# First part of a two-block transformer kernel: VectorE operands in PSUM, one activation table in the opening, split row loads, new slots

## The chip, the cores and the metric

One core of one Trainium2 chip. The time is the device time of one launch in microseconds (us). Before the change it was 2034.73 us, the median of 3 runs (2034.38 to 2038.0).

## The reference

The input is x of 8 x 256 x 128, called eight samples of 256 tokens here. Two blocks follow each other. `_layernorm(x) * (1 + scale) + shift` and a gate come from the condition c by an adaLN modulation; a gate's magnitude is kept at 0.25 or more. The kernel computes, for each sample:

```python
# block 0, attention: features relu(q rw), relu(k rw); no softmax
kv  = einsum('bhsf,bhsd->bhfd', kp, v); out = (qp kv) / (qp sum(kp) + EPS)
# block 0, experts: 8 dense experts, gelu, weights of the two best gates
h = gelu(x @ W_in[e] + b_in[e]); out += combine[e] * (h @ W_out[e] + b_out[e])
# block 1, sparse attention over x itself
probs = softmax(x x^T / sqrt(D)); vacuum = probs < 0.01
attended = (kept probs / their sum) x;   + 0.01 * sum(vacuum probs) * W
# block 1, "late": 6 layers of local attention (16 heads of 64, windows of 32,
# l2-normed and rotated q and k), each with a gated gelu feed-forward
```

The modulation multiplies silu(c) by a 128 x 768 matrix for each block.

## The kernel before

Activations stand transposed, 128 features on the partitions, 256 tokens of one sample in the free dimension. Three kinds of jobs run: `attention(b)` (block 0's attention), `experts(b)` (experts and then the sparse attention and the last layer norm of the first part) for b = 0 to 7, and `late(u)` for 48 units, u = 8 * layer + sample. The first part is the 16 jobs of the first two kinds; the late part follows, and the two overlap a little, since sample 0 can start before sample 7 is done.

Each engine has its own program, and in it the order of all jobs is written by hand through slots: a job is a generator that moves from step to step at given slots (`PE_A`, `ACT_B`, `DVE_AT` and so on), and `interleave` merges the jobs by slot number. The slots are no times: they only give the order of instructions on each engine. Engines meet through semaphores (`wait_ge`, `then_inc`). `settle` is a wait of an engine for its own last instruction.

PSUM has eight banks. In the first part `Banks.take` hands them out in a ring: the ninth request gets the first bank again, and TensorE waits until that bank's user has signalled. In the late part three banks form such a ring.

The opening: ACT issues 13 small loads of rows (biases, gains and the two conditions, `row_loads`), copies the four turned parts of x out of PSUM (L887), and waits for `cols`, all 105 rows turned by TensorE in one transposition (L432). Then `silu` on ACT (L899) with its own activation table, six products per block (`modulation`, L439), and on VectorE some fifteen small instructions from L1196 to L1207 that build scale, shift and gate. Only then does VectorE enter `attention(0)`, since it waits for `mod` ahead of the first layer norm. Block 1's silu and modulation and the constants `wcT` and `wsum` are made in `prepare_block1` when `experts(0)` starts.

A layer norm is one pattern on four engines: TensorE mean (L459), VectorE subtraction (L1230), ACT square (L906), TensorE variance (L463), ACT ln and exp (L910, L911), VectorE product with that (L1234, both operands in SBUF) and scale and shift (L1242, SBUF to SBUF). L893 is the load of the table that has ln and exp.

The sparse attention: TensorE scores of sample b in the bank `s1` (L614), VectorE maximum (L1383), ACT exp into the SBUF tile `e_prob` (L996), VectorE division by the sum (L1390), twice two selections with sums (L1395, L1397; signal `sp`), TensorE transposition (L623), ACT copy (L1002), TensorE product (L631), VectorE L1413 and L1416.

In the late part, per half c of a unit: ACT copies q and k (L1019, `raw`) and squares them (L1027), VectorE sums (L1455, `ss`), turns them by sine (L1468, `sin`), POOL turns them by cosine (L1665, `cos`) and adds both (L1674, `add`), VectorE normalises (L1476, `nrm`), TensorE transposes (L690, `tqk`). The softmax is `smax` (L1489, L1490), `exp` (L1060), `ssum`. The tables of the rotation are made by L1439 and L1440 in unit 0.

SP issues loads of x, of weights and constants; POOL splits weights into two parts (L1603, L1604) chunk by chunk, and SP loads chunk i only when chunk i - 2 is split.

## Time and profile before

| what | before |
|---|---|
| median of 3 runs | 2034.73 us |
| the profiled execution's own time | 2035.73 us |
| its span, first to last instruction | 2034.4 us |
| TensorE busy | 1875.6 us (92%) |
| VectorE, ACT, POOL busy | 1576.5, 1606.5, 1068.7 us |
| mean granted TensorE clock | 0.984 |

The span is what the rows below add up to; 1.3 us of the profiled execution lie around it. Busy TensorE time is modelled from pipelined instructions, so it counts a slowly clocked or queued product as busy. The first part takes about the first fifth of the span.

### The profile page before, as it was taken

The page shows a single profiled execution, that of the slowest core. Times are in us where ns is not written, and L with a number is a line of the kernel's source. Part 1 is how long each engine was busy: PE and PEld are TensorE (multiplying, and loading weights), DVE is VectorE, ACT ScalarE, POOL GpSimd, SP SyncE. Part 2 cuts the span into 40 slices and gives each one's busy share as a digit, 9 for nine tenths or more (in the row PEclk, how much of TensorE's full clock was granted, in tenths as well). Part 3 has the DMA queues.
Part 4 walks back from the last instruction along what each step waited for, and adds up shares of the span by engine and source line. Part 5 has one row for each costly group of instructions (what it writes and reads, how often), then busy time and mean ns, then how long its engine had stood idle before and what let it go on. Part 6 is the DMA issues. An engine that isn't in the chain of part 4 may idle for free.

```text
span 2034.4 us, 78899 instructions
## 1 busy us (share of the span) xinstructions
PE 1875.6 (92%) x34796; PEld 1571.9 (77%) x34796; DVE 1576.5 (77%) x2244; ACT 1606.5 (79%) x2840; POOL 1068.7 (53%) x523
## 2 busy tenths in 40 slices
PE   4999999768999999999999999999999999999986
PEld 3789998656777777778778778777778787878775
DVE  4565655568888888878788888888888888889874
ACT  2577777557888888888888888888888888888864
POOL 3100000256567666677575766656765668666430
PEclk9899999889999999999999999999999999999999
DMA  5000000023434333243433343333434334342331
GB/s 170 7 12 5 5 7 6 2 81 87 115 82 126 98 106 112 80 127 85 114 94 115 92 127 100 107 104 90 122 91 124 88 94 129 98 115 80 103 80 43
DMA packets 119822, 174.01 MB, mean 86 GB/s; under 512 B 25303, under 2 KB 44346, under 8 KB 119482
## 3 DMA queue, kind: packets, MB, share of 16 engines
q1 hardware_dynamic: 119308, 168.92, 30.0%
q8 instruction: 275, 4.51, 0.9%
q14 instruction: 65, 0.53, 0.1%
q10 hardware_dynamic: 174, 0.05, 0.0%
HBM read 117.54 MB, written 51.38 MB: 83 GB/s over the span
## 4 chain that ended last, share of the span: by engine, by line
PE 63%; DVE 20%; issue 7%; POOL 5%; ACT 4%; ACTq 0%; DMA 0%; POOLq 0%; DVEq 0%
PE bank L690 7%; PE s_pair L712 6%; PE bank L667 5%; PE bank L669 5%; PE bank L668 5%; DVE bank L1455 5%; DVE rt L1476 4%; DVE t L1468 4%; PE o_pair L741 4%; PE bank L724 4%; PE bank L753 3%; PE bank L862 3%; DVE sm L1489 2%; PE s_pair L594 2%; POOL rt L1665 2%
## 5 line engine op out<-in xcount | busy, mean ns | idle before, releaser
L1665 POOL TENSOR_TENSOR rt<-raw,rot 128x1024 f32<-128x1024 f32 x192 | 456.0, 2375 | 318.1 <-PE bank L690 259.0
L1674 POOL TENSOR_TENSOR rt<-rt,t 128x2048 f32<-128x2048 f32 x96 | 439.4, 4578 | 184.3 <-DVE t L1468 180.2
L667 PE MATMUL bank<-wqkv_hi,xs 128*128 128x512 f32 x576 | 252.8, 439 | 7.6 <-ACT vn L1036 2.8
L1489 DVE TENSOR_REDUCE sm<-s_pair 128x16 f32<-128x1024 f32 x96 | 117.6, 1225 | 182.1 <-PE s_pair L712 178.8
L1019 ACT ACTIVATE raw<-bank 128x512 f32<-128x512 f32 x384 | 229.1, 598 | 29.2 <-PE bank L669 5.0
L690 PE MATMUL bank<-const,rt 128*128 128x128 f32 x1536 | 209.2, 279 | 32.7 <-DVE rt L1476 29.5
L668 PE MATMUL bank<-wqkv_lo,xs 128*128 128x512 f32 x576 | 228.5, 397 | 1.2 <-issue 1.2
L1476 DVE TENSOR_TENSOR rt<-rt,bank 128x2048 f32<-128x2048 f32 x96 | 219.6, 2288 | 12.1 <-POOL rt L1674 9.1
L669 PE MATMUL bank<-wqkv_hi,xs 128*128 128x512 f32 x576 | 228.8, 397 | 0.0
L1468 DVE TENSOR_TENSOR t<-raw,bank 128x1024 f32<-128x1024 f32 x192 | 224.8, 1211 | 0.6
L1455 DVE TENSOR_REDUCE bank<-t 128x32 f32<-128x2048 f32 x96 | 219.4, 2286 | 5.8 <-ACT t L1027 5.7
L690 PEld LDWEIGHTS bank<-const,rt 128*128 128x128 f32 x1536 | 170.7, 142 | 68.4 <-issue 49.2
L1027 ACT ACTIVATE t<-raw 128x2048 f32<-128x2048 f32 x96 | 184.8, 1926 | 7.6 <-POOL rt L1674 6.5
L840 PE MATMUL bank<-oT,wo 128*128 128x256 f32 x768 | 173.7, 379 | 0.9 <-DVE hh L1514 0.9
L712 PE MATMUL s_pair<-kT,qT 64*32 64x64 f32 x12288 | 157.1, 226 | 13.9 <-issue 13.9
L712 PEld LDWEIGHTS s_pair<-kT,qT 64*32 64x32 f32 x12288 | 131.8, 106 | 46.0 <-issue 35.6
L741 PE MATMUL o_pair<-v,pT 64*32 64x64 f32 x12288 | 147.8, 225 | 17.8 <-issue 17.8
L741 PEld LDWEIGHTS o_pair<-v,pT 64*32 64x32 f32 x12288 | 128.5, 105 | 45.8 <-issue 45.8
L840 PEld LDWEIGHTS bank<-oT,wo 128*128 128x128 f32 x768 | 145.4, 190 | 22.7 <-DVE hh L1514 1.1
L1053 ACT ACTIVATE kT<-bank 128x512 f32<-128x512 f32 x192 | 104.8, 596 | 72.8 <-PE bank L690 69.8
L1047 ACT ACTIVATE qT<-bank 128x512 f32<-128x512 f32 x192 | 104.3, 597 | 69.8 <-PE bank L690 69.8
L1633 POOL TENSOR_TENSOR e_hs<-e_h_b,e_hs 128x256 fp32r<-128x256 f32 x8 | 5.8, 727 | 283.2 <-ACT e_hs L959 283.2
(363 smaller groups left out, 4467.0 us busy)
## 6 DMA issues: line engine op xcount, KB each, us to landing
v<-v_rows SPq DMA_DIRECT2D x288, 256.0 KB, 4.5
v_rows<-vn SPq DMA_DIRECT2D x192, 256.0 KB, 3.8
v<-v_rows SPq DMA_DIRECT2D x96, 192.0 KB, 3.4
wraw<-in_L_ffn_Wqkv_dram SPq DMA_DIRECT2D x36, 256.0 KB, 3.1
wo<-in_L_ffn_Wo_dram SPq DMA_DIRECT2D x6, 512.0 KB, 4.8
wraw<-in_L_ffn_W_in_dram SPq DMA_DIRECT2D x8, 256.0 KB, 3.7
w_out<-in_L_ffn_W_out_dram SPq DMA_DIRECT2D x8, 256.0 KB
wraw<-in_L_ffn_W_dram SPq DMA_DIRECT2D x12, 170.5 KB, 2.3
```

The costliest lines, as they stand in the source:

```text
L667: pe.matmul(bank[:, :], hi, w[0][:, :], start=True, stop=False)
L668: pe.matmul(bank[:, :], hi, w[1][:, :], start=False, stop=False)
L669: return pe.matmul(bank[:, :], lo, w[0][:, :], start=False, stop=True)
L690: e = pe.transpose(bank[:, i * P:(i + 1) * P], k.rt_r[c][:, at:at + P], k.ident)
L712: e = pe.matmul(k.s_pair[WIN * g:WIN * (g + 1), at:at + 2 * WIN], qT[rows, hp, WIN * g:WIN * (g + 1)], k.kT_r[u % 2][rows, hp, k0:k0 + 2 * ...
L741: e = pe.matmul(k.o_pair[WIN * g:WIN * (g + 1), at:at + DH], k.pT_r[c][rows, hp, WIN * g:WIN * (g + 1)], k.v2_r[c][rows, g, hp * DH:(hp + ...
L840: e = pe.matmul(bank[:, 0:S], k.wo[:, n, :], k.oT_r[u % 2][:, n, :], start=(n == 0), stop=(n == INNER // P - 1))
L1455: dve.tensor_reduce(k.rn_p[c], heads(k.t2[:, :]), AX.X, ALU.add).then_inc(s["sq_sum"], 1)
L1468: e = dve.tensor_tensor(pairs(k.t2[:, part]), pairs(k.raw_r[c][:, part])[:, :, ::-1, :], sinv, ALU.mult)
L1476: dve.tensor_tensor(v, v, k.rn_p[c].unsqueeze(2).to_broadcast([P, 2 * HEADS, DH]), ALU.mult)\
L1665: e = pool.tensor_tensor(heads(k.rt_r[c][:, part]), heads(k.raw_r[c][:, part]), cosv, ALU.mult)
L1674: pool.tensor_tensor(k.rt_r[c][:, :], k.rt_r[c][:, :], k.t2[:, :], ALU.add).then_inc(s["rot_add"], 1)
```

## The change

It changes the first part's code and every slot table. The arithmetic stays the same but for the form of silu and of the gates.

- Rows: `bq, bk, bo, c0, c1` get a tile `rows_f` and a signal of their own (`ld_first`, 5 loads); the other 8 loads go to `rows_m`, five of them ahead of the copies of x, three behind. POOL clears `rows_m` instead of VectorE.
- Opening: ACT loads one table (ln, exp) at once. silu is computed as c / (1 + exp(-c)): exp on ACT, three instructions on VectorE, for both blocks together. The mean and the subtraction of `attention(0)` stand ahead of the modulation; TensorE turns the rest of x and the early rows after the first mean, and makes modulation(0) after the first variance. The gate needs six VectorE instructions instead of fifteen.
- PSUM operands: ACT writes the exp of a layer norm and the exp of the sparse softmax back into their banks, and VectorE's next steps read and write there. The variance's bank is held until the layer norm's end, the bank `s1` until `sp`.
- Loads: block 1's modulation matrix and `w_c` come behind the first two chunks; the eight `w_out` tiles alternate with chunks and have two signals of their own.
- Slots: all tables are new.

```diff
-ATTENTION_START, ATTENTION_SPACING = 0, 40
-EXPERTS_START, EXPERTS_SPACING = 63, 40
-LATE_START, LATE_SPACING = 399, 32
+ATTENTION_START, ATTENTION_SPACING = 2, 40
+EXPERTS_START, EXPERTS_SPACING = 65, 40
+LATE_START, LATE_SPACING = 398, 32
...
-DVE_B = dict(ln_sq_b=0, ln_sd_b=12, ln_out_b=15, top2=18, weights=19, combine=30, expert0=33, expert1=35, expert2=38,
-             expert3=44, expert4=44, expert5=54, expert6=54, expert7=56, expert8=59, moe_out=60, ln_sq_c=60,
-             ln_sd_c=71, ln_out_c=77, scores=77, exp=81, threshold=81, spT=92, attend=96, back=97, ln_sq_d=97,
-             ln_sd_d=102, ln_out_d=102)
...
+DVE_B = dict(ln_sq_b=0, ln_sd_b=9, ln_out_b=13, top2=19, weights=20, combine=22, expert0=30, expert1=40, expert2=43,
+             expert3=48, expert4=53, expert5=57, expert6=58, expert7=60, expert8=64, moe_out=67, ln_sq_c=67,
+             ln_sd_c=80, ln_out_c=82, scores=82, exp=84, threshold=84, spT=95, attend=99, back=102, ln_sq_d=102,
+             ln_sd_d=111, ln_out_d=111)
...
-ACT_AT = dict(xs=0, qk00=9, qk01=10, qk02=11, qk03=12, sq0=20, qk10=20, norm0=29, qk11=30, qk12=35, qk13=35, sq1=36,
-              norm1=41, v00=41, v01=44, v10=46, v11=48, tqk00=49, tqk01=49, tqk02=61, tqk03=61, tqk10=64, tqk11=64,
-              tqk12=65, tqk13=67, exp0=73, tp00=77, tp01=78, exp1=96, tp10=100, tp11=102, to00=104, to01=104,
-              to10=114, to11=117, xf=129, lnsq=135, rstd=137, gelu0=150, gelu1=150, gelu2=153)
-DVE_AT = dict(ss0=15, sin0=21, nrm0=29, ss1=33, sin1=38, nrm1=58, smax0=60, ssum0=76, smax1=79, oa0=91, ssum1=92,
-              oa1=108, z_mid=124, xc=127, hn=134, hh0=144, hh1=145, hh2=145, z_out=160)
...
+ACT_AT = dict(xs=0, qk00=7, qk01=9, qk02=9, qk03=10, sq0=14, qk10=16, norm0=25, qk11=28, qk12=33, qk13=33, sq1=34,
+              norm1=39, v00=39, v01=42, v10=43, v11=43, tqk00=43, tqk01=45, tqk02=55, tqk03=56, tqk10=61, tqk11=63,
+              tqk12=65, tqk13=65, exp0=71, tp00=75, tp01=75, exp1=92, tp10=98, tp11=99, to00=101, to01=103, to10=108,
+              to11=112, xf=128, lnsq=132, rstd=134, gelu0=146, gelu1=148, gelu2=151)
+DVE_AT = dict(ss0=17, sin0=26, nrm0=32, ss1=38, sin1=40, nrm1=60, smax0=64, ssum0=75, smax1=81, oa0=93, ssum1=95,
+              oa1=106, z_mid=126, xc=133, hn=136, hh0=146, hh1=146, hh2=153, z_out=162)
...
+    def prepare_block0():
+        turn_x(1)
+        columns(0, k.rows_f, FIRST_ROWS, (s["ld_first"], 16 * k.n_first_dma), ("silu", 2))
+        turn_x(2)
+        turn_x(3)
...
+        if b == 0 and tag == "a":
+            prepare_block0()
         yield from t.to("ln_sq_" + tag)
-        bank = bank_for(("var", tag, b), "ln_sd_" + tag, b + 1)
+        bank = bank_for(("var", tag, b), "ln_out_" + tag, b + 1)
         pe.wait_ge(s["ln_sq_" + tag], b + 1)
         pe.matmul(bank[:, 0:S], k.ones_d[:, :], xsq, start=True, stop=True).then_inc(s["ln_var_" + tag], 1)
+        if b == 0 and tag == "a":
+            modulation(0)
...
-        bank = bank_for(("s1", b), "exp1", b + 1)
+        bank = bank_for(("s1", b), "sp", b + 1)
...
+    exp_ln()
+    for dst, src in k.first_loads:
+        act.dma_start(dst, src).then_inc(s["ld_first"], 16)
+    act.wait_ge(s["ones"], 2)
+    for dst, src in k.row_loads[:ROWS_BEFORE]:
         act.dma_start(dst, src).then_inc(s["ld_rows"], 16)
     for q in range(NT // P // 4):
         act.wait_ge(s["pe_x"], q + 1)
         act.activation(k.xT[:, q * 512:(q + 1) * 512], k.work.at["x", q][:, :], ACT.Copy).then_inc(s["xT"], 1)
+        if q == 1:
+            at = ROWS["c0"][0]
+            act.wait_ge(s["cols"], 1)
+            act.activation(k.work.at["cols", 0][:, at:at + 2 * B], k.cols[:, at:at + 2 * B], ACT.Exp, scale=-1.0)\
+                .then_inc(s["silu"], 1)
+    for dst, src in k.row_loads[ROWS_BEFORE:]:
+        act.dma_start(dst, src).then_inc(s["ld_rows"], 16)
...
-        act.activation(sq, sq, ACT.Exp, scale=-0.5).then_inc(s["ln_sd_" + tag], 1)
+        act.activation(k.work.at["var", tag, b][:, 0:S], sq, ACT.Exp, scale=-0.5).then_inc(s["ln_sd_" + tag], 1)
...
+    def silu():
+        at = ROWS["c0"][0]
+        c, e = k.cols[:, at:at + 2 * B], k.work.at["cols", 0][:, at:at + 2 * B]
+        dve.wait_ge(s["silu"], 1)
+        settle(dve.tensor_scalar(e, e, 1.0, None, ALU.add))
+        settle(dve.reciprocal(e, e))
+        dve.tensor_tensor(k.silu[:, :], c, e, ALU.mult).then_inc(s["silu"], 1)
...
+        dve.tensor_copy(mod[:, 0::3, :], raw[:, 0::3, :])
+        dve.tensor_scalar(mod[:, 1::3, :], raw[:, 1::3, :], 1.0, None, ALU.add)
+        settle(dve.tensor_scalar(mag, raw[:, 2::3, :], -1.0, 0.25, ALU.mult, ALU.max))
+        settle(dve.tensor_tensor(mag, mag, raw[:, 2::3, :], ALU.max))
+        settle(dve.scalar_tensor_tensor(out=twice, in0=raw[:, 2::3, :], scalar=0.0, in1=mag,
+                                        op0=ALU.is_ge, op1=ALU.mult))
+        dve.scalar_tensor_tensor(out=mod[:, 2::3, :], in0=twice, scalar=2.0, in1=mag,
+                                 op0=ALU.mult, op1=ALU.subtract).then_inc(s["mod"], 1)
...
-        settle(dve.tensor_tensor(xc, xc, sd, ALU.mult))
+        if b == 0 and tag == "a":
+            dve.wait_ge(s["mod"], 1)
+        settle(dve.tensor_tensor(xn, xc, xn, ALU.mult))
...
-        dve.tensor_scalar(dst, xc, gain, shift, ALU.mult, ALU.add).then_inc(s["ln_out_" + tag], 1)
+        dve.tensor_scalar(dst, xn, gain, shift, ALU.mult, ALU.add).then_inc(s["ln_out_" + tag], 1)
...
-        for c in range(TC):
-            e = dve.tensor_scalar(pr[:, c, :], pr[:, c, :], one(RS, c), None, ALU.mult)
-        settle(e)
         if b:
             dve.wait_ge(s["pe_spT"], b)
         for c in range(TC):
-            settle(dve.scalar_tensor_tensor(out=spb[:, c, :], in0=pr[:, c, :], scalar=THRESH, in1=pr[:, c, :],
-                                            op0=ALU.is_lt, op1=ALU.mult, accum_out=one(VAC, c)))
-            e = dve.scalar_tensor_tensor(out=spb[:, c, :], in0=pr[:, c, :], scalar=THRESH, in1=pr[:, c, :],
-                                         op0=ALU.is_ge, op1=ALU.mult, accum_out=one(SPS, c))
+            e = dve.tensor_scalar(spb[:, c, :], pr[:, c, :], one(RS, c), THRESH, ALU.mult, ALU.is_ge)
+        settle(e)
+        for c in range(TC):
+            e = dve.scalar_tensor_tensor(out=spb[:, c, :], in0=pr[:, c, :], scalar=one(RS, c), in1=spb[:, c, :],
+                                         op0=ALU.mult, op1=ALU.mult, accum_out=one(SPS, c))
+        settle(e)
+        for c in range(TC):
+            e = dve.scalar_tensor_tensor(out=pr[:, c, :], in0=pr[:, c, :], scalar=one(RS, c), in1=spb[:, c, :],
+                                         op0=ALU.mult, op1=ALU.subtract, accum_out=one(VAC, c))
         e.then_inc(s["sp"], 1)
...
+    sp.dma_start(k.wmod[1][:, :], a["L1_wmod"]).then_inc(s["ld_wmod1"], 16)
+    sp.dma_start(k.w_c[:, :], a["L1_attn_W"]).then_inc(s["ld_moe"], 16)
     for e in range(NE):
+        if 2 + e < NE:
+            load_chunk(2 + e)
         sp.dma_start(k.w_out[:, e, :, :], a["L0_ffn_W_out"][e].rearrange("(m p) n -> p m n", p=P))\
-            .then_inc(s["ld_moe"], 16)
+            .then_inc(s[f"ld_out{e // (NE // 2)}"], 16)
```

## Rows read from the trace of the kernel before

**Rows 1.** Windows: us, then busy us of PE, PEld, DVE, ACT, POOL, PEclk, DMA, GB/s.

```profile
66.00:335.00 269.00, 268.15 (x2430) 242.86 (x2431) 156.50 (x502) 203.17 (x417) 14.61 (x18) 1.00 0.03 7
...
400.00:475.00 75.00, 45.51 (x795) 36.11 (x796) 56.76 (x58) 40.50 (x68) 48.57 (x23) 0.78 0.24 68
...
500.00:1960.00 1460.00, 1391.53 (x29285) 1152.22 (x29284) 1242.08 (x1421) 1242.01 (x2131) 954.18 (x434) 1.00 0.38 103
```

**Rows 2.** Timeline of the opening: start, us, engine, line, operation, [idle before, releaser].

```profile
8.07 2.07 ACT L887 ACTIVATE xT<-bank 128x512 f32<-128x512 f32 x4
10.81 0.43 PE L432 MATMUL s_pair<-const,rows_m 105*128 105x105 f32 x1 [2.24 <-DMA rows_m<-in_L_c_dram]
11.94 2.70 PE L439 MATMUL s_pair<-silu,wmod 128*128 128x8 f32 x12 [0.69 <-ACT silu L899]
14.68 0.21 DVE L1196 COPY mod<-s_pair 128x48 f32<-128x48 f32 x1 [3.12 <-PE s_pair L439]
21.43 0.42 DVE L1230 TENSOR_TENSOR e_ln_a<-xT,o_pair 128x256 f32<-128x256 f32 x1
...
23.67 1.28 ACT L893 ACT_TABLE_LOAD   x1 [1.30 <-PE o_pair L463]
...
26.38 0.72 DVE L1242 TENSOR_SCALAR e_h_a<-e_ln_a,mod 128x256 f32<-128x256 f32 x1
```

**Rows 3.** The same timeline, from the end of attention(0) to the first expert.

```profile
44.18 0.43 DVE L1304 TENSOR_TENSOR xT<-xT,e_oT 128x256 f32<-128x256 f32 x1
...
52.61 1.06 PE L459 MATMUL bank<-xT,ones_d 128*128 128x256 f32 x2
...
66.62 0.39 PE L584 MATMUL bank<-e_hs,w_in_hi 128*128 128x256 f32 x1
```

**Rows 4.** Timeline of the steady first part around one use of the bank s1.

```profile
117.39 1.03 PE L614 MATMUL bank<-e_h_c 128*128 128x256 f32 x4
119.69 1.95 PE L594 MATMUL s_pair<-w_out,e_hid 128*128 128x128 f32 x16
...
123.33 1.95 PE L594 MATMUL bank<-w_out,e_hid 128*128 128x128 f32 x16
...
125.64 0.08 DVE L1397 DVE_READ_ACCUMULATOR e_sp<-e_prob 128x1 f32 x1
```

**Rows 5.** VectorE instructions by line: ns min/median/max, first and last start.

```profile
L1390 DVE TENSOR_SCALAR e_prob<-e_prob,e_small x16: 346/353/4652, 123.4 to 399.4; 128x256 f32<-128x256 f32 x16
L1242 DVE TENSOR_SCALAR e_h_b<-e_ln_b,mod x8: 411/412/414, 59.6 to 342.1; 128x256 f32<-128x256 f32 x8
L1302 DVE TENSOR_SCALAR e_oT<-s_pair,cols,mod x5: 543/544/546, 108.4 to 276.3; 128x256 f32<-128x256 f32 x5
L1476 DVE TENSOR_TENSOR rt<-rt,bank x96: 2286/2289/2290, 411.4 to 1965.6; 128x2048 f32<-128x2048 f32 x96
```

**Rows 6.** Timelines of POOL, VectorE, TensorE and ACT where the parts meet.

```profile
394.60 4.77 POOL L1665 TENSOR_TENSOR rt<-raw,rot 128x1024 f32<-128x1024 f32 x2 [9.65 <-DVE rot L1440]
396.99 7.10 DVE L1390 TENSOR_SCALAR e_prob<-e_prob,e_small 128x256 f32<-128x256 f32 x2
399.45 4.49 POOL L1674 TENSOR_TENSOR rt<-rt,t 128x2048 f32<-128x2048 f32 x1
410.85 1.09 PE L623 MATMUL s_pair<-const,e_sp 128*128 128x128 f32 x4 [16.61 <-DVE e_sp L1397]
412.59 1.91 ACT L1027 ACTIVATE t<-raw 128x2048 f32<-128x2048 f32 x1
420.63 4.58 POOL L1674 TENSOR_TENSOR rt<-rt,t 128x2048 f32<-128x2048 f32 x1 [10.22 <-DVE t L1468]
```

**Rows 7.** One late unit: ACT's timeline, then TensorE in the critical chain.

```profile
1021.81 0.58 ACT L1019 ACTIVATE raw<-bank 128x512 f32<-128x512 f32 x1
1022.28 1.05 ACT L1060 ACTIVATE p<-p 128x1024 f32<-128x1024 f32 x1
...
1023.62 0.87 PE bank L690 x8
```

More of the change, by code:

```diff
@@ L200 @@
 SIGNALS = (
-    "ones zero rf xT cols silu mod cst wsum w_split "
+    "ones rf xT cols silu mod cst wsum w_split "
     "pe_x pe_setup "
@@ L423, in pe_program, with turn_x @@
     pe.wait_ge(s["ld_ident"], 16)
-    for q in range(NT // P // 4):
+    def turn_x(q):
         bank = bank_for(("x", q), "xT", q + 1)
@@ L429, in pe_program, with columns @@
         e.then_inc(s["pe_x"], 1)
-    bank = bank_for("cols", "cols", 1)
-    pe.wait_ge(s["ld_rows"], 16 * k.n_rows_dma)
-    pe.transpose(bank[:, 0:NROWS], k.rows_m[0:NROWS, :], k.ident[0:NROWS, 0:NROWS]).then_inc(s["pe_setup"], 1)
+    turn_x(0)
+    def columns(n, rows, count, loaded, free):
+        bank = bank_for(("cols", n), *free)
+        pe.wait_ge(*loaded)
+        pe.transpose(bank[:, 0:count], rows[0:count, :], k.ident[0:count, 0:count]).then_inc(s["pe_setup"], 1)
     def modulation(n):
@@ L880, in shifted @@
         return act.activation(dst[DH:P, 1:S], src[DH:P, 0:S - 1], ACT.Copy)
-    act.wait_ge(s["zero"], 1)
-    for dst, src in k.row_loads:
-        act.dma_start(dst, src).then_inc(s["ld_rows"], 16)
-    for q in range(NT // P // 4):
-        act.wait_ge(s["pe_x"], q + 1)
-        act.activation(k.xT[:, q * 512:(q + 1) * 512], k.work.at["x", q][:, :], ACT.Copy).then_inc(s["xT"], 1)
-    act.wait_ge(s["cols"], 1)
     table = {"set": None}
@@ L1212, in dve_program, with columns @@
-    modulation(0)
+    def columns(n, first, count, ready):
+        dve.wait_ge(s["pe_setup"], ready)
+        dve.tensor_copy(k.cols[:, first:first + count], k.work.at["cols", n][:, 0:count]).then_inc(s["cols"], 1)
+    def silu():
[5 more added lines that the diff above has]
+        dve.tensor_tensor(k.silu[:, :], c, e, ALU.mult).then_inc(s["silu"], 1)
@@ L1411, in experts @@
             dve.wait_ge(s["pe_atT"], b)
+        parts = [bank[:, c * D:(c + 1) * D] for c in range(TC)]
         for c in range(TC):
-            e = dve.tensor_scalar(o[:, c, :], bank[:, c * D:(c + 1) * D], one(SPS, c), None, ALU.mult)
+            e = dve.tensor_scalar(parts[c], parts[c], one(SPS, c), None, ALU.mult)
         settle(e)
         for c in range(TC):
-            e = dve.scalar_tensor_tensor(out=o[:, c, :], in0=k.wsum[:, :], scalar=one(VAC, c), in1=o[:, c, :],
+            e = dve.scalar_tensor_tensor(out=o[:, c, :], in0=k.wsum[:, :], scalar=one(VAC, c), in1=parts[c],
                                          op0=ALU.mult, op1=ALU.add)
@@ L1779, in sp_program @@
     load_down(0)
-    for i in range(2, NE + 2 + NCHUNK_LATE):
+    for i in range(NE, NE + 2 + NCHUNK_LATE):
         load_chunk(i)
@@ L1873, in row_loads @@
     rows("c1", a["L1_c"], B)
-    return out
+    return first, out
 class Chunks:
```

169 lines of the change are left out of this document (80 added, 89 removed).

## Prediction

> **What bounds the kernel now.** I read the windows first, then the timelines of the places where TensorE is not full, then the chain of waits of one late unit. The reader is to see three stretches in the windows [rows 1]. From 66 to 335 us TensorE is busy 268.15 of 269.00 us at clock 1.00: there only TensorE's own work counts, and faster VectorE instructions are worth nothing. Ahead of 66 us it waits for chains through all engines [rows 2, 3]. Where the parts meet, 400 to 475 us, it is idle 29.5 us, at a mean clock of 0.78. In the late part, 500 to 1960 us, it is idle 68.5 of 1460 us, about 1.5 us in each unit of some 32 us (48 units in 1559 us). The change can gain in the opening and at the meeting point, can lose in the full stretch, and can do either in the late part through the slots alone.
>
> **The opening, before the first h.** Today the rows land at 10.81, all 13 loads of them. The modulation products end at 11.94 + 2.70 = 14.64, and VectorE works on gates from 14.68 until the first subtraction at 21.43. The first h is there at 26.38 + 0.72 = 27.10, that is 5.7 us after that subtraction, with a table load of 1.28 in between [rows 2].
>
> After the change the subtraction needs only the first part of x. ACT issues 10 loads ahead of the copies instead of 13, and has no table load there; its first copy, at 8.07 behind 13 issues and a load of the length of 1.28, comes at about (8.07 - 1.28) x 10 / 13 = 5.2, and with the table load somewhere ahead I take 5.6, the mean at 7 and the subtraction at 8. The first rows (five loads, issued first) I take as landed at 8.5: nearest row 10.81, for the last of 13 loads. TensorE then turns them and the last two parts of x until 10.5; ACT waits for the turned columns between its second and third copy, so exp, two copies (2.07 / 4 each), three load issues (6.8 x 3 / 13 = 1.6) and the square queue behind that wait: the square comes at 12.8. So the variance is made at 13.3 to 14.5 and the modulation, queued behind it, until 14.5 + 2.7 = 17.2. VectorE's six gate instructions take 1.6 (0.21 each, and four waits for itself). Two layer norm instructions of 0.43 and 0.72 at most end h at 19.9. **Gain 7.2 us.** If the rows land no sooner than now, 10.81, everything from the transposition on is 2.3 later and the gain is 4.9. If the modulation were done when it is now, 14.64, it is 9.7. The new wait of VectorE for `mod`, ahead of the product, has nothing but this chain behind it.
>
> **The preparation of block 1.** From the end of attention(0), 44.18 + 0.43 = 44.6, to the mean of experts(0) at 52.61 pass 8.0 us, and the first expert starts at 66.62 [rows 3]. Gone are silu's table load (1.28), the wait for silu, half of the gate instructions (some 1 us) and the reload of the ln and exp table for that layer norm (1.28); new are one transposition of the late rows and its copy, 0.43 and some 0.3, partly beside the products. The rest of the waits stands. I take 3.3 us; bounds 1.3 (one load) and 5. SP's `w_out` loads now queue behind the waits for splits; they are needed from the first expert on, at 56, and at some 3 us per pair of loads from 15 on (an estimate) all are in by 40. Opening together: **-10.5 us**, from -6 to -14.
>
> **The full stretch.** TensorE's own work stays the same. Two banks are held longer. The bank s1 is written by 117.39 + 1.03 = 118.4, and `sp`, which now frees it, comes at 125.7, 7.3 us later [rows 4]. The new VectorE order has the same six instructions, but two of them read PSUM, which adds some 0.5 us: 7.8. In the new order eight requests behind s1 are two experts (three banks each), the variance of the next experts job and the first of four banks for the q features. One expert takes about (123.33 - 119.69) - 0.43 = 3.2 us [rows 4], so the eighth request comes after 6.4 + 0.4 = 6.8 us. That is 1.0 us too soon, in seven samples at most, and everything of TensorE is queued behind that wait: +7. It is 0 if ACT and VectorE run a microsecond ahead. I take the middle, **+4 us**. The variance's bank is asked for again after eight requests, too, but its owner needs only a further 0.8 us of VectorE, ahead of that point; I cost it at nothing, and it costs the same per sample if VectorE is behind.
>
> A VectorE instruction also gets slower by the move: a scale and shift out of SBUF takes 412 ns, one with a PSUM operand of the same size 544 ns [rows 5]. 32 of the first and 16 of L1390 (353 ns) move: 32 x 0.13 + 16 x 0.19 = 7.2 us of VectorE, bounds 0 and 7.2. VectorE is busy 156.50 of 269 us in the full stretch, so I take nothing for it beyond the 0.5 us in the sum above. The Trainium skill, VectorE: DVE Perf Modes, section Why PSUM operands drop a tier, speaks against the change here: PSUM has one read port for VectorE, so a fp32 `tensor_scalar` with a PSUM operand falls back to one element a cycle. By the page each of those 48 would take up to twice its time, and on the path they would make the sum 19 us longer, an estimate. The rows price the step at 544 / 412 = 1.3 for the scale and shift and at most 544 / 353 = 1.5 for L1390 [rows 5], and the measured durations are used.
>
> **Where the parts meet.** For the last sample the two divisions take 7.10 us together instead of 2 x 0.353, and the six instructions from 396.99 to 410.8 take 13.8 us, where the same six of sample 0 run from 123.4 to 125.7, in 2.3 [rows 4 to 6]: POOL's rotation and sum run beside them, 394.60 to 399.4 and 399.45 to 403.9 [rows 6]. TensorE stood idle 16.61 us for it. With PSUM operands I take them at 3.4 us, since L1476, one operand in PSUM, keeps to 2286 to 2290 ns in all 96 cases, those beside POOL's work among them [rows 5]. What is late next is POOL's own sum at 403.94: ACT's second square, which came at 412.59 behind the selections' copy, needs just that. So [rows 6] 412.59 - 403.94 = 8.65 us go, and the next POOL sum, now at 420.63, follows by the same amount. The new slots put VectorE's rotation of unit 0 ahead of the last sample's h, and ACT's first square ahead of its squares: POOL's 394.60 moves to about 391.5, 3 us more, against 2 us by which the last sample's own chain is later, which is now covered. **-11.7 us**; bounds -5 (another wait takes half) and -17 (all of the idle 16.61).
>
> **The late part.** Slots swap neighbours: on TensorE one transposition pair, the feed-forward's down product and the mean; on VectorE the layer's end ahead of the subtraction; on ACT the second exp ahead of the copy of `qk11`; SP's and POOL's splits and loads move at layer ends only. I find no wait on which TensorE stands that any of these moves by more than its slack, and take 0, with 8 us either way (0.17 us per unit).
>
> **Sum:** -10.5 + 4 - 11.7 + 0 = -18.2 us on the profiled span of 2034.4, which becomes 2016.2; with the 1.3 us around it 2017.5 against 2035.73. The median is 1.0 below that execution: 2016.5.
>
> **Rivals.**
> (1) The bank s1 stalls in full and the layer norm banks with it: 2 us in each of seven samples, 14 instead of 4. For it speaks that TensorE has no idle time to hide it; against it, that the swap of slots may have put VectorE's part ahead. 2026.5.
> (2) The opening gives only what the gate instructions gave, because the small loads land late behind x: -5 instead of -10.5: 2022. For it: ten loads share the queues with 1 MB of x.
> (3) The meeting point gains more or less: POOL's sum is not next, but the idle 16.61 us go as a whole, or the rotation ahead of h costs what it gains: 2011 or 2023.
> (4) Slower: ACT's second exp, 1.05 us, ahead of the copy of `qk11`. The copy now starts at 1021.81 and takes 0.58; behind the exp it ends at about 1023.4, and the transpositions at 1023.62 hold the second that reuses its bank 0.4 later [rows 7]. The margin is 0.6 us. If ACT is later than in this unit by that, TensorE waits in every unit; it decides from 0.39 us per unit on (18.2 / 47), and with 0.45 us it is +21: 2038.
> (5) The slower PSUM reads lie on the path, 7.2 us of VectorE in all: 2023.7. The Trainium skill's section named above states the rule behind this rival. VectorE's 58% share in the full stretch speaks against it.
> (6) The change does not do what it says: VectorE still waits beside POOL at the meeting point, 2025.
>
> **How the numbers follow.** A measurement of this kernel tells about 0.2%, 4 us, from no change. Chances: forecast (2010 to 2021) 0.42; (1) 0.12; (2) 0.12; (3) 0.14; (4) 0.08; (5) 0.04; (6) 0.04; 0.04 left for more gain than I count. The range takes the forecast's own bounds, (2), (3), (5), (6) and most of (1): 2001 to 2030. Faster by over 4 us is all but (4) and a part of (1): 0.88. Within 4 us 0.05, slower 0.07.
>
> **What the changed profile would show.** The first subtraction near 8 and the first h near 20; the first expert product near 56; no table load between the start and that expert's gelu; the full stretch without TensorE waits on VectorE or, if I am right about s1, about seven waits of under 1 us ahead of the q features; the six selections of the last sample in 3 to 4 us, and POOL's second sum some 20 us earlier than 420.63; the same late part, shifted. The forecast is wrong if the late units take another time than now, or if the first expert starts at 60 or later.

## The result, and the profile after

Two sets of 20 runs have medians of 2036.1 us before and 2041.92 us after. The ratio of the two, with its 95% interval, is 1.0022 [1.0012, 1.0033]: slower by about 4.5 us, just past the 0.2% that the prediction took as the bound. The forecast was 2016.5, with a range of 2001 to 2030 and 0.88 on faster. It was wrong in sign and outside its range. The profiled execution has a span of 2039.2 us and took 2040.55.

The windows of the changed kernel (columns as in [rows 1], with the number of instructions behind each busy time) show where TensorE lost time:

```profile
66.00:335.00 269.00, 255.29 (x2322) 230.25 (x2318) 157.99 (x487) 195.30 (x396) 14.66 (x18) 1.00 0.03 7
...
400.00:475.00 75.00, 49.22 (x748) 38.21 (x749) 54.51 (x61) 41.57 (x75) 45.26 (x22) 0.78 0.24 69
500.00:1960.00 1460.00, 1383.58 (x29307) 1155.03 (x29289) 1239.89 (x1417) 1240.29 (x2125) 955.64 (x435) 1.00 0.37 103
```

In the full stretch TensorE is busy 255.29 of 269 us, where it was 268.15 [rows 1]: 13 us of new idle time, at an unchanged clock of 1.00. The rest of the text follows four milestones: the end of `attention(0)`, the residual additions that end each sample's experts (`x2`), VectorE's first rotation product of the late part (`nrm0`, L1507), and the first late output (unit 0's last step on VectorE, L1600). The table is put together from the starts in VectorE's timeline of both kernels, in us; `x2` (L1395) has eight starts, one per sample.

```
                 attention(0)  x2 first   x2 last   last-first   nrm0    nrm0 - x2 last   first late output
before               44.18      103.08    382.50      279.42    411.44       28.94             535.53
after                34.12       94.95    386.54      291.59    412.00       25.46             538.22
difference          -10.06       -8.13     +4.04      +12.17     +0.56       -3.48              +2.69
```

The books balance: -8.1 at the first `x2`, +12.2 over seven samples, -3.5 to `nrm0`, +2.1 from there to the first late output is +2.7; another +2.1 comes in 47 further units, and the span is 4.8 longer.

**The opening** came as it was said, and somewhat better up to the first h. These are lines of the changed kernel's timeline, columns as in [rows 2]:

```profile
0.74 1.28 ACT L903 ACT_TABLE_LOAD   x1 [0.74 <-PEq L1965]
...
7.58 0.42 DVE L1252 TENSOR_TENSOR e_ln_a<-xT,bank 128x256 f32<-128x256 f32 x1 [7.58 <-PE bank L470]
...
12.86 2.08 PE L445 MATMUL o_pair<-silu,wmod 128*128 128x8 f32 x12
...
16.52 0.54 DVE L1271 TENSOR_SCALAR e_h_a<-o_pair,mod 128x256 f32<-128x256 f32 x1
...
55.52 0.39 PE L599 MATMUL bank<-e_hs,w_in_hi 128*128 128x256 f32 x1
```

The first subtraction starts at 7.58 instead of 21.43, the first h is there at 17.06 instead of 27.10, and the first expert's product starts at 55.52 instead of 66.62 [rows 2, 3].

**The full stretch** has waits on TensorE that were not there. TensorE's waits from 100 to 335 us in the changed kernel (us in total, times, longest):

```profile
PE bank L580 <- DVE e_gate L1368: 4.8, 5, 1.3
PE s_pair L517 <- DVE s_pair L1427: 4.7, 5, 0.9
PE s_pair L611 <- DVE zT L1271: 1.9, 4, 0.5
```

and the longest of the kernel before in the same view:

```profile
PE bank L601 <- DVE e_acc L1362: 0.4, 1, 0.4
```

The second line is the bank `s1`, which the q features of `attention` (L517) ask for again. Its own place, from the timelines of TensorE and VectorE in the changed kernel:

```profile
240.84 1.03 PE L631 MATMUL s_pair<-e_h_c 128*128 128x256 f32 x4
...
248.14 0.60 PE L476 MATMUL bank<-e_ln_b,ones_d 128*128 128x256 f32 x2
249.67 0.48 PE L517 MATMUL s_pair<-e_qkT,w_rf 32*128 32x256 f32 x2 [0.93 <-DVE s_pair L1427]
```

The scores end at 241.87; `sp` releases the bank 7.8 us later, and the q features that reuse it wait 0.93 us.

From the first to the last `x2` TensorE's waits add up to 14.3 us: 5.6 for gates (L580, six times), 6.3 for `s1`, 2.4 for banks of the layer norms.

**The meeting point** has short selections and a new hold. POOL, VectorE and TensorE in the changed kernel, columns as in [rows 6]:

```profile
393.67 4.77 POOL L1696 TENSOR_TENSOR rt<-raw,rot 128x1024 f32<-128x1024 f32 x2 [4.68 <-DVE rot L1471]
398.52 4.53 POOL L1705 TENSOR_TENSOR rt<-rt,t 128x2048 f32<-128x2048 f32 x1
405.41 0.72 POOL L1718 TENSOR_TENSOR xs<-zT,xs 64x256 fp32r<-64x256 f32 x1 [2.36 <-ACT xs L897]
...
406.92 4.79 POOL L1696 TENSOR_TENSOR rt<-raw,rot 128x1024 f32<-128x1024 f32 x2
419.12 4.56 POOL L1705 TENSOR_TENSOR rt<-rt,t 128x2048 f32<-128x2048 f32 x1 [7.41 <-DVE t L1499]
```

```profile
400.15 2.93 DVE L1412 TENSOR_SCALAR e_small<-e_small 128x2 f32<-128x2 f32 x1
...
404.36 0.88 DVE L1420 TENSOR_SCALAR e_sp<-s_pair,e_small 128x256 f32<-128x256 f32 x2
...
407.20 2.10 DVE L1431 TENSOR_SCALAR e_small<-e_small 128x2 f32<-128x2 f32 x1
...
409.42 2.32 DVE L1433 TENSOR_SCALAR e_small<-e_small 128x2 f32<-128x2 f32 x1
...
412.00 2.29 DVE L1507 TENSOR_TENSOR rt<-rt,bank 128x2048 f32<-128x2048 f32 x1
```

```profile
407.31 1.09 PE L640 MATMUL s_pair<-const,e_sp 128*128 128x128 f32 x4 [5.37 <-DVE s_pair L1427]
```

The 256-wide selections no longer wait. But three `tensor_scalar`s over **two** elements in each partition (128x2), which scale the negated maximum, add 1e-9 and multiply by 0.01, take 2.93, 2.10 and 2.32 us. How long they take elsewhere stands in VectorE's groups by line (ns min/median/max):

```profile
L1420 DVE TENSOR_SCALAR e_sp<-s_pair,e_small x14: 474/480/484, 113.3 to 404.8; 128x256 f32<-128x256 f32 x14
L1423 DVE SCALAR_TENSOR_TENSOR e_sp<-s_pair,e_small,e_sp x14: 478/482/485, 114.2 to 405.7; 128x256 f32<-128x256 f32 x14
...
L1412 DVE TENSOR_SCALAR e_small<-e_small x8: 169/170/2926, 110.2 to 400.1; 128x2 f32<-128x2 f32 x8
L1416 DVE RECIPROCAL e_small<-e_small x8: 165/166/166, 113.1 to 404.2; 128x2 f32<-128x2 f32 x8
L1431 DVE TENSOR_SCALAR e_small<-e_small x8: 169/170/2100, 116.1 to 407.2; 128x2 f32<-128x2 f32 x8
L1432 DVE RECIPROCAL e_small<-e_small x8: 165/166/166, 116.3 to 409.3; 128x2 f32<-128x2 f32 x8
L1433 DVE TENSOR_SCALAR e_small<-e_small x8: 147/149/2324, 116.4 to 409.4; 128x2 f32<-128x2 f32 x8
```

The instructions with a PSUM operand keep to 484 and 485 ns; the two-element `tensor_scalar` out of SBUF goes from 170 to 2926. For L1420 these rows are no test, since POOL idles from 403.05 to 405.41, just where the last pair runs. The test is the same instruction in r11_last_sample_again, described below, where it runs from 389.81 on and POOL's pair from 387.41 to 392.20:

```profile
L1437 DVE TENSOR_SCALAR e_sp<-s_pair,e_small x2: 474/479/484, 389.8 to 390.2; 128x256 f32<-128x256 f32 x2
```

Each of the three slow ones ends where an instruction of POOL ends: 400.15 + 2.93 = 403.08 is the end of the sum L1705 (403.05), 407.20 + 2.10 = 409.30 is the middle of the pair L1696, and 409.42 + 2.32 = 411.74 its end (406.92 + 4.79 = 411.71). `nrm0` comes behind both, at 412.00. The Trainium skill, SBUF — State Buffer, section Who interferes with whom, has this as an exclusive lock on the port pair that VectorE's two-port mode shares with GpSimd, with the second to issue blocked for the whole instruction; these rows agree. The prediction had priced this wait on the wide instructions only. The reciprocal L1432 runs between two of them, beside the same pair, and keeps to 166 ns.

### The profile page after: what moved, and what is told of

The parts are those of the page before. It is cut to its first block, busy times and chain, and to the rows that moved or that the text cites. A ratio compares the mean times of both kernels' runs of the same rounds, so it can differ in the third digit from the quotient of the medians.

```text
span 2039.2 us, 78883 instructions
## 1 busy us (share of the span) xinstructions
PE 1874.3 (92%) x34797; PEld 1579.7 (77%) x34797; DVE 1573.3 (77%) x2229; ACT 1604.3 (79%) x2835; POOL 1070.2 (52%) x524
## 3 DMA queue, kind: packets, MB, share of 16 engines
q8 instruction: 275, 4.51, 0.9%
## 4 chain that ended last, share of the span: by engine, by line
PE 60%; DVE 21%; issue 8%; ACT 6%; POOL 5%; DMA 0%; ACTq 0%; POOLq 0%; DVEq 0%; SPq 0%
PE bank L707 7%; PE s_pair L729 6%; PE bank L684 6%; PE bank L686 5%; PE bank L685 5%; DVE rt L1507 4%; DVE bank L1486 4%; PE o_pair L758 4%; DVE t L1499 4%; PE bank L741 4%; PE bank L770 3%; PE bank L879 3%; DVE sm L1520 2%; POOL rt L1705 2%; POOL rt L1696 2%
## 5 line engine op out<-in xcount | busy, mean ns | idle before, releaser
L1696 POOL TENSOR_TENSOR rt<-raw,rot 128x1024 f32<-128x1024 f32 x192 | 456.4, 2377 | 328.0 <-PE bank L707 288.2
L1705 POOL TENSOR_TENSOR rt<-rt,t 128x2048 f32<-128x2048 f32 x96 | 439.7, 4580 | 163.1 <-DVE t L1499 159.0
L707 PE MATMUL bank<-const,rt 128*128 128x128 f32 x1536 | 219.3, 281 | 34.6 <-DVE rt L1507 28.2
L1507 DVE TENSOR_TENSOR rt<-rt,bank 128x2048 f32<-128x2048 f32 x96 | 219.6, 2288 | 13.2 <-POOL rt L1705 10.0
L729 PEld LDWEIGHTS s_pair<-kT,qT 64*32 64x32 f32 x12288 | 132.3, 106 | 42.7 <-issue 32.1
L1066 ACT ACTIVATE qT<-bank 128x512 f32<-128x512 f32 x192 | 110.1, 599 | 67.2 <-PE bank L707 67.2
```

Source lines behind the costliest of these rows:

```text
L707: e = pe.transpose(bank[:, i * P:(i + 1) * P], k.rt_r[c][:, at:at + P], k.ident)
L729: e = pe.matmul(k.s_pair[WIN * g:WIN * (g + 1), at:at + 2 * WIN], qT[rows, hp, WIN * g:WIN * (g + 1)], k.kT_r[u % 2][rows, hp, k0:k0 + 2 * ...
L1507: dve.tensor_tensor(v, v, k.rn_p[c].unsqueeze(2).to_broadcast([P, 2 * HEADS, DH]), ALU.mult)\
L1696: e = pool.tensor_tensor(heads(k.rt_r[c][:, part]), heads(k.raw_r[c][:, part]), cosv, ALU.mult)
L1705: pool.tensor_tensor(k.rt_r[c][:, :], k.rt_r[c][:, :], k.t2[:, :], ALU.add).then_inc(s["rot_add"], 1)
```

## The experiments

Each was run beside the kernel before on the same chip; the medians of the kernel before on the three chips are 2036.8, 2033.99 and 2036.93 us, so ratios are compared, not medians. "Stretch" is the last `x2` less the first; "meeting" is `nrm0` less the last `x2`. Both come from one profile each, in us. What one profile can tell is seen from e8 and r11, which are the same kernel: they differ by 0.85 us in the stretch, by nothing at the meeting point, and by 2.5 us at the first late output.

```
kernel                      ratio [95%]               stretch   meeting   first late output
before                                                279.42    28.94     535.53
after                       1.0022 [1.0012, 1.0033]   291.59    25.46     538.22
e1_code_old_slots           1.0023 [1.0008, 1.0038]   301.31    22.45     540.39
e2_slots_old_code           1.0021 [1.0004, 1.0037]   282.21    25.85     541.38
e3_small_off_port           0.9961 [0.9946, 0.9976]   293.29    18.35     531.29
e4_s1_free_at_exp           0.9965 [0.9951, 0.9980]   285.96    25.88     530.20
e5_ln_banks_free            1.0001 [0.9987, 1.0015]   287.66    25.41     533.22
e6_all_banks_free           0.9953 [0.9937, 0.9969]   282.03    25.85     528.61
e7_opening_alone            0.9953 [0.9936, 0.9969]   279.69    28.92     526.65
e8_last_sample_old_slots    0.9941 [0.9923, 0.9959]   279.96    21.37     520.12
r9_last_sample_new_slots    0.9925 [0.9903, 0.9947]   281.96    18.16     520.97
r10_last_small_only         0.9953 [0.9938, 0.9968]   280.21    28.26     526.71
r11_last_sample_again       0.9926 [0.9903, 0.9948]   280.81    21.37     522.60
```

**Code and slots taken apart.** The first run is the changed code with the slot tables of before, the second the code of before with the new tables; the diff is the tables alone.

```diff
-PE_B = dict(ln_sq_b=6, ln_sd_b=6, ln_out_b=12, ...
+PE_B = dict(ln_sq_b=6, ln_sd_b=6, ln_out_b=15, ...
```

> The changed code with all slot tables of the kernel before. Changed kernel's profile: x2 of the samples comes 44.5 us apart instead of 42.0, and three TensorE waits per sample stand there: 0.9 to 1.3 us for the bank s1, 0.9 for the gate weights, 0.5 for the bank of the last layer norm. Theory S (order): most of the loss is the new slots, so here the spacing is 42 to 42.5 and the kernel keeps the opening's gain of 8 to 10 us: 2024 to 2030 where the kernel before has 2036. Theory B (banks held longer): the wait for s1 is there in any order, the spacing is 43 to 43.5, and the kernel is at 2031 to 2037. Theory D (VectorE slower by its PSUM reads): spacing 44 to 44.5 as in the changed kernel, 2040.

> The code before with all new slot tables. Theory S: the spacing of x2 is 43.5 to 44.5 with no gain in the opening, 2044 to 2052. Theory B: spacing 42.0 to 42.5 and 2036 to 2040. In both the opening's first h stays at 27.

Neither half is the gain or the loss: both are slower than before. The first came to 2041.21 us, near the number of theory D, but with the cause of theory B, and with 45.8 us from `x2` to `x2` where none had more than 44.5. The second came to 2041.54, between the two ranges, with nearly the spacing of theory B (42.2 to 42.7). With the old slots the changed code stretches to 301.31, and TensorE's waits from 100 to 335 us name all three held banks:

```profile
PE bank L599 <- DVE e_h_b L1271: 7.8, 5, 1.6
PE bank L599 <- DVE bank L1427: 4.7, 5, 0.9
PE s_pair L599 <- DVE e_h_c L1271: 2.6, 5, 0.5
```

L1271 is the end of a layer norm, which now frees the variance's bank, with 1.6 us a sample ahead of `experts(b)` and 0.5 us for the sparse block. So the new slots repair much of what the held banks cost: 9.7 us of the stretch. Of these, 2.7 are lost again ahead of the first `x2` (94.95 against 92.30). By themselves, with the old code, they cost 2.8 us in the stretch, at the gates (this is the view of the second run), and give 3.1 at the meeting:

```profile
PE bank L565 <- DVE e_gate L1341: 4.6, 5, 1.2
```

That alone would be no loss. But the first `x2` comes 3.0 us later too (106.04), and 3.2 more pass from `nrm0` to the first late output, which is 5.85 us behind that of the kernel before.

At the meeting point this run shows something that the prediction did not see. VectorE in e2_slots_old_code, and POOL's second pair there:

```profile
406.03 0.62 DVE L1390 TENSOR_SCALAR e_prob<-e_prob,e_small 128x256 f32<-128x256 f32 x2
...
408.90 2.44 DVE L1397 SCALAR_TENSOR_TENSOR e_sp<-e_prob 128x256 f32<-128x256 f32 x1
...
411.38 2.18 DVE L1401 TENSOR_SCALAR e_small<-e_small 128x2 f32<-128x2 f32 x1
```

```profile
408.65 4.89 POOL L1665 TENSOR_TENSOR rt<-raw,rot 128x1024 f32<-128x1024 f32 x2
```

The two divisions, all out of SBUF, take 0.62 us together instead of 7.10 [rows 6]. The new slots alone put them where POOL idles (its sum ends at 404.72, its next instruction starts at 407.08). So slots and PSUM operands save in part the same wait. What is left ends with POOL's second pair, at 413.54 here and at 411.71 in the changed kernel, and `nrm0` follows 0.6 and 0.3 us later.

**The small instructions.** The changed kernel without the three two-element `tensor_scalar`s on VectorE. ACT scales the negated maximum, 0.01 goes into the summed weights, and the addition of 1e-9 is left out.

```diff
+        settle(act.activation(sm[:, 0:TC], sm[:, 0:TC], ACT.Copy, scale=-scale))
...
-        settle(dve.tensor_scalar(sm[:, SPS], sm[:, SPS], 1e-9, None, ALU.add))
-        dve.reciprocal(sm[:, SPS], sm[:, SPS])
-        settle(dve.tensor_scalar(sm[:, VAC], sm[:, VAC], 0.01, None, ALU.mult))
+        settle(dve.reciprocal(sm[:, SPS], sm[:, SPS]))
```

> The changed kernel without its three two-element VectorE instructions that go from SBUF to SBUF (L1412, L1431, L1433): ACT makes the negative maximum, 0.01 is put on the constant wsum, and the addition of 1e-9 is left out. In the changed kernel they took 2.93, 2.10 and 2.32 us beside POOL at the meeting point instead of 0.17. Theory M (they are what ate the meeting point's gain): VectorE's normalisation of unit 0 starts 5 to 6 us earlier after x2 of the last sample and the kernel is 4 to 6 us faster than the changed one: 2036 to 2038. Rival (the chain through POOL's sum and the squares sets the time anyway): 0 to 2 us, 2040 to 2042.

`nrm0` comes 18.35 us behind the last `x2` instead of 25.46: 7.1 us, close to the 2.93 + 2.10 + 2.32 = 7.35 that the three took, and more than the 5 to 6 expected. The first late output is 6.9 us earlier. The ratio falls from 1.0022 to 0.9961, which is 12 us; the 5 beyond what the milestones show are not explained. The stretch stays long, at 293.29, as it should where no bank is freed sooner.

**The held banks one by one.** The first gives the sparse softmax back to SBUF and frees `s1` at `exp1`; the second gives the layer norms back and keeps `s1` in PSUM; the third does both, so that opening, loads and new slots are left.

```diff
-        bank = bank_for(("s1", b), "sp", b + 1)
+        bank = bank_for(("s1", b), "exp1", b + 1)
```

The other two choose by two functions that the runs after them use as well (these are the lines of the second; the third has `HOLD_S1 = lambda b: False`).

```diff
+HOLD_LN = lambda tag, b: False
+HOLD_S1 = lambda b: True
...
-        bank = bank_for(("var", tag, b), "ln_out_" + tag, b + 1)
+        bank = bank_for(("var", tag, b), ("ln_out_" if HOLD_LN(tag, b) else "ln_sd_") + tag, b + 1)
...
-        bank = bank_for(("s1", b), "sp", b + 1)
+        bank = bank_for(("s1", b), "sp" if HOLD_S1(b) else "exp1", b + 1)
```

> The changed kernel with the sparse softmax as before: exp goes to SBUF, the bank s1 is freed at exp, VectorE selects out of SBUF. New slots and opening stay. Theory B: the wait for s1 (0.9 to 1.3 us per sample) goes, the spacing falls from 44.5 to 43.2, but at the meeting point the selections again wait for POOL (about 14 us instead of 3): 2036 to 2044 in all. Theory S: another wait takes its place, spacing 44 or more.

> The changed kernel with one part undone: the normalisations of the first part write to SBUF again, so the bank of the mean square is free at ln_sd instead of at ln_out; the sparse softmax in PSUM, the opening and the new slots stay. Theory A (held banks cost TensorE a wait in each sample, each by itself): the wait before the matmul that follows the small sparse scores (0.93 us in the changed kernel) stays, the 0.5 us wait behind VectorE's multiply by 1/sd goes, x2 spacing 42.2 to 42.8 us per sample against 42.85, total 2034 to 2042. Rival B (only the bank of the scores matters): spacing unchanged at 42.85 within 0.2, total as changed (2041). Rival C (either bank held is enough to break a chain, freeing one frees all): spacing falls to 42.0 as without the hold of the scores, total about 2030.

> The changed kernel with the normalisations and the sparse softmax both in SBUF as before: what is left of the change is the opening, the order of the loads, the new slots and the two attention outputs whose banks are held no longer than before. Theory A (held banks and new slots each have a price): spacing about 41.5 us per sample (41.0 of before plus 0.45 that the new slots cost the code before), last x2 at 377 to 379, first norm0 of the late part 26 to 29 us behind it, total 2026 to 2030. Rival B (the slots cost nothing once the banks are free): spacing 41.0, last x2 at 373, total about 2024. Rival C (late part decides; what the first part gains is not kept): total within 2 us of 2030, the same as with the scores' bank freed alone.

The stretches add up. From 282.03 with nothing held, the layer norm banks alone make 285.96 (+3.9), `s1` alone 287.66 (+5.6), both 291.59 (+9.6). In the waits the line of the q features is gone in the first run, and the line behind the layer norm's end in the second; with all freed only the gates remain of the repeated waits. That view of e6_all_banks_free:

```profile
PE bank L584 <- DVE e_gate L1376: 4.7, 5, 1.3
PE bank L615 <- ACT e_hid L1001: 1.2, 1, 1.2
```

A wait in the view isn't always its full size in time. The waits for `s1` add up to 6.1 us between the first and the last `x2` of e5_ln_banks_free, for 5.6 us of stretch; those for the gates to 5.6 us in e6_all_banks_free and to 0.8 in the run below, whose stretch is only 2.3 us shorter.

The first run missed its expectation: 2036 to 2044 us, with 14 us for the selections out of SBUF, and it took 2029.65 with the meeting at 25.88. The reason is the one of e2_slots_old_code: it has the new slots, and its divisions out of SBUF take 0.61 us together. The second landed as theory A said (2034.16), the third below it (2022.41 for 2026 to 2030).

Of the totals, both freed together are worth 1.0022 - 0.9953 = 0.0069, or 14 us, more than the 9.6 us of the stretch. The rest I can't place: first late outputs differ by 9.6, and what comes behind varies by some 10 us from profile to profile with the same late slots.

**The opening alone.** e6_all_banks_free with the old slot tables. Against the kernel before it has the new opening, the early rows and the order of the loads.

> The kernel before with the new opening, the early rows and the order of the loads, its old slots kept and everything else of the first part in SBUF as before. Theory A (the opening's 10 us pass through unchanged): first x1 at 34 to 35, spacing 41.0, last x2 at 372 to 374 (382.5 before), first norm0 28 to 29 us later, total 2025 to 2029 against 2036. Rival B (the earlier start is lost where loads of the experts or the first waits of the old slots hold it): last x2 above 378, total above 2031.

The gain passes through whole, as theory A said: the last `x2` is at 372.72 (9.8 us earlier), the first late output 8.9 earlier, the ratio 0.9953, which is 9.6 us. So opening and loads alone are 14 us faster than the changed kernel. And the stretch (279.69 against 279.42) shows that an earlier start costs the samples nothing.

**PSUM operands where no sample follows.** For the last sample no later sample waits for a bank. This kernel is the opening alone, plus PSUM operands only there (the layer norm of the sparse block's output for the last two samples), plus the small `tensor_scalar`s of the last sample kept off VectorE; ACT adds 1e-9, so nothing is left out. The factor 0.01 goes into the summed weights, for all samples.

```diff
-HOLD_LN = lambda tag, b: False
-HOLD_S1 = lambda b: False
+HOLD_LN = lambda tag, b: b == B - 1 or (tag == "d" and b == B - 2)
+HOLD_S1 = lambda b: b == B - 1
...
+        if b == B - 1:
+            act.activation(sm[:, 3 * TC:4 * TC], sm[:, 3 * TC:4 * TC], ACT.Identity, bias=k.eps9[:, :]).then_inc(s["sps"], 1)
```

> The opening alone (as in the run beside it), and for the last sample only, behind which no sample waits for a bank: normalisations and sparse softmax read PSUM as in the change, and the three two-element tensor_scalars of its sparse softmax are kept off VectorE (ScalarE scales the negated maximum and adds 1e-9, and 0.01 is folded into the summed weights). Same output as the reference; old slots. Theory A (the meeting point is held by VectorE's SBUF-only instructions behind POOL): spacing 41.0 as with the opening alone, first norm0 18 to 22 us behind the last x2 instead of 28.9, total 5 to 9 us below the opening alone, 2017 to 2022. Rival B (the meeting point is held elsewhere once the first late unit's units on POOL are reached): norm0 earlier, but the first late output no earlier than with the opening alone within 2 us, total equal to it.

> The last-sample kernel with old slots once more, beside the two runs that differ from it by one part, so that all three share the chip and the runs of the kernel before. Expected 0.9941 of the time before within 0.002; spacing 41.1 and first norm0 21.4 us behind the last x2, both within 0.3.

Ratios 0.9941 and 0.9926, ahead of both kernels and with the output kept; 21.37 us at the meeting in both. Against the opening alone (0.9953) the intervals overlap; the gain over it rests on the first late output, 6.5 and 4 us earlier. The 2020.72 us of e8 were 4.2 below the opening alone in the same set, where 5 to 9 were expected. That VectorE no longer waits for a port there, only for POOL's result, can be seen in its timeline (r11_last_sample_again): its product waits with nothing to do until POOL's sum is there.

```profile
396.89 2.29 DVE L1540 TENSOR_TENSOR rt<-rt,bank 128x2048 f32<-128x2048 f32 x1 [4.06 <-POOL rt L1739]
```

```profile
392.28 4.51 POOL L1739 TENSOR_TENSOR rt<-rt,t 128x2048 f32<-128x2048 f32 x1
```

392.28 + 4.51 = 396.79, 0.1 us ahead of `nrm0`. With the old slots POOL's own chain is the floor now. In e1_code_old_slots, with the small instructions in place, one of them took 4.17 us, to 415.11; POOL's sum ended at 415.09 there and `nrm0` came at 416.06, one microsecond above that floor.

**Which half of it.** The same kernel with the last sample's PSUM operands taken back and only the small instructions kept away, and the same kernel with the new slots.

> The last-sample kernel with old slots, its PSUM operands taken back: normalisations and sparse softmax of the last sample work in SBUF as before, and only the three two-element tensor_scalars stay off VectorE. Theory A (what holds the meeting point is whichever SBUF-only tensor_scalar is issued while POOL works; the 256-wide one takes over): a tensor_scalar of 256 columns lasts 6 to 7 us again, first norm0 28 to 29 us behind the last x2, total as with the opening alone. Rival B (the small ones were the whole hold): norm0 at 21 to 23 us, total as the last-sample kernel.

> The last-sample kernel (opening; PSUM operands and no two-element tensor_scalar on VectorE only in the last sample) with the new slots in place of the old. Theory A (new slots cost 0.4 us per sample through the gates' wait and give 3 us at the meeting point): spacing 41.4 to 41.5, first norm0 18 to 19 us behind the last x2 (21.4 with the old slots), total 2018 to 2023, equal to the old slots within 2 us. Rival B (the new slots are the worse in the late part too): total above 2024.

Without PSUM operands the wide instructions are blocked instead (VectorE in r10_last_small_only):

```profile
387.33 7.11 DVE L1450 TENSOR_SCALAR e_prob<-e_prob,e_small 128x256 f32<-128x256 f32 x2
...
396.01 2.55 DVE L1455 SCALAR_TENSOR_TENSOR e_sp<-e_prob 128x256 f32<-128x256 f32 x1
```

The meeting takes 28.26 us again and the ratio is 0.9953, that of the opening alone, as theory A said. So freeing the wide ones and freeing the small ones are not two gains that add, and how they combine hangs on the slots. The meeting in us, from the table above:

```
                                        old slots   new slots
SBUF operands, small ones on VectorE      28.9        25.9
PSUM operands, small ones on VectorE      22.5        25.5
SBUF operands, small ones elsewhere       28.3        not run
PSUM operands, small ones elsewhere       21.4        18.2 (18.4 in e3)
```

Under the old slots PSUM operands alone nearly reach POOL's floor. Under the new ones POOL's first pair starts 7.1 us behind the last `x2` instead of 12.1, and the divisions run in POOL's gap even out of SBUF; there PSUM operands win 0.4 us, since the small instructions wait for POOL's sum and second pair all the same. With both kept away POOL's sum ends at 395.64 in r9_last_sample_new_slots and `nrm0` comes at 397.29, held by the last sample's own selections. The new slots (0.9925) and the old (0.9926) end alike: 3.2 us are won at the meeting, some 2.6 are lost ahead of the first `x2` and 1 to 2 in the stretch, and what is left is below what these runs can tell.

## Why the prediction was wrong

- **The opening, -10.5 us: right.** -10.06 at the end of `attention(0)`, -11.1 at the first expert, 9.6 in the total of e7_opening_alone. Inside it the split was off: I had 7.2 ahead of the first h and 3.3 in block 1's preparation, and it was 10.0 and about 1. By the first `x2`, 3.0 of the 11.1 us are lost again. With the old slots it keeps 10.8 us in e1 and 10.05 in e7, and the new slots alone lose 3.0 there in e2, so that loss is the slots', a term that I put at nothing. The terms that I took too long were the square (set at 12.8, it came at 11.86), the variance behind it (0.70 us instead of 1.2) and the modulation, 2.08 us instead of 2.70 and done at 14.94 instead of 17.2.
- **The full stretch, +4 us: this step failed; it was +12.2.** The bank `s1` was right as a mechanism and nearly exact as a case: I had 7.8 us held against 6.8 us until asked for, and so 1.0 us; it was 7.8 and a wait of 0.93. But I took half of seven such waits as my term, where TensorE pays each time: 5.6 us by e5 and e6. The variance's bank, "I cost it at nothing", is 3.9 us by e4 and e6: I had looked at the bank's owner ("a further 0.8 us of VectorE") and not at how soon TensorE asks for it again: in one sample that variance is written by 186.06, its bank is asked for at 192.00 and free at 192.47. The order of the slots in the full stretch, which I didn't cost at all, is 2.3 us, by e6 against e7, or 2.8, by e2 against before. 5.6 + 3.9 + 2.3 = 11.8 of 12.2. So of the 8.2 us by which the step was off, 3.9 are the variance's bank, 2.3 the slots, 1.6 the half, and 0.4 are left over. Rival (1), with 14 us, had this size and got 0.12.
- **The meeting point, -11.7 us: this step failed; it was -3.5, and -1.4 at the first late output.** The step added 8.65 us for the selections and 3 us for the slots. Each came to something by itself, 6.5 us for the PSUM operands under the old slots (22.45 in e1 against 28.94) and 3.1 us for the slots (25.85 in e2), but on top of the new slots the PSUM operands were worth 0.4 (25.46 against 25.85). The step said "With PSUM operands I take them at 3.4 us", and they took 3.0, from 404.16 to 407.16. Two things were wrong. It stopped at the six wide instructions and left out the small ones that stand ahead of them and behind them, 7.35 us in all, 7.1 of which e3 gives back. And it took the whole wait of the kernel before as there to be won, where the new slots alone already bring the divisions from 7.10 to 0.62 us. Rival (6) named the first mechanism, VectorE still waiting beside POOL, with 0.04. For the slots I had POOL 3 us earlier and the sample 2 us later; it was 5.0 and 3.3, so that the net of 3 is in part luck. That what is late next is POOL's own sum was right as a floor under the old slots: the last-sample kernels reach it.
- **The slower PSUM reads** cost nothing that shows by itself. The scale and shift of the first h takes 0.54 us, the 544 ns that was priced, and so 1.3 times the 412 ns out of SBUF [rows 5] and not up to twice. VectorE was busy 157.99 instead of 156.50 us in the window of the full stretch, while TensorE's new idle time stands at bank releases. So rival (5) is not what is seen; but the added time of those reads is a part of how long each bank is held, and no run takes the two apart.
- **The late part, 0 ± 8:** right as far as it can be told. From the first late output to the end of the span it is 1501.0 against 1498.9 us. Over all profiles of the table the six with the old slots have 1491.8 to 1498.9, on average 1495.5, and the seven with the new ones 1491.4 to 1501.0, on average 1496.0. ACT's second exp ahead of the copy, rival (4), opens no wait that would repeat in 47 units: half a microsecond on average is not 21.
- **The sum:** -8.1 + 12.2 - 1.4 + 2.1 = +4.8 in the spans, where the forecast had -18.2. The two failed steps are off by 8 and 10 us in the same direction, each past its own bound (+7 and -5), and the range left no room for both at once.

## What to carry to other kernels

Moving an operand into PSUM took these VectorE instructions out of GpSimd's way (480 ns each beside POOL, where the pair out of SBUF took 7.10 us), but it holds a bank. Where TensorE is full and takes banks in turn, what is held beyond the turn is paid in every iteration: do it only where nothing follows that wants the bank. Before counting on a port being free, list every SBUF-to-SBUF `tensor_scalar` in the chain, however small, since one of two elements waits as long as one of 256. Price a wait that recurs at its full size times its count, and take that as the upper end: here it was 6.1 us for 5.6 with `s1`, and 4.8 for 2.3 with the gates. Before two gains are added, ask whether both remove the same wait.

## What was not expected of the hardware

- A `tensor_scalar` over 128x2 fp32 out of SBUF takes 170 ns alone and 2.10, 2.32, 2.93 and (with the old slots) 4.17 us when issued beside a GpSimd `tensor_tensor`; it ends within 0.04 us of that instruction's end. A reciprocal over the same two elements is not held: in r11_last_sample_again it starts at 389.61, within POOL's pair (387.41 + 4.79), and takes 0.16 us.
- With the same late slots the late part takes 1491.8 to 1498.9 us in six profiles and 1491.4 to 1501.0 in seven, so up to 10 us, as much as the effects studied here. One and the same kernel, e8 and r11, has its first late output at 520.12 and 522.60. In a single profile only milestones ahead of it can be compared, and differences under a microsecond in the stretch not even there.
- The same opening ends `attention(0)` at 34.1 to 37.2 us in eleven profiles with it. Part of the 10 us gained there is thus spread over 3 us from run to run; what varies was not looked into.
